# A hybrid block of layers: block 0's states ahead of block 1's turning, maxima in three pairs of PSUM banks in turn, one mix of the last mixer later

## The chip, the core and the metric

The kernel runs on one core of one Trainium2 chip. A core has five engines that run at the same time, each with its own in-order queue: TensorE (PE, matrix products and transposes; its weight loads are listed as PEld), VectorE (DVE), ScalarE (ACT), GpSimd (POOL), and SyncE (SP), which here only issues transfers. They meet in semaphores. PE writes its results into PSUM, eight banks of 128 partitions x 512 float32. The metric is the device time of one execution in microseconds (us); lower is better.

## The reference, cut to what matters

Input is `x` of 2 sequences x 2048 tokens x 256 channels. Four layers follow, each added to its input:

```
x = x + ssm(layernorm(x))                # a = -softplus(A_diag); state = a*state + B u; LN(gelu(C state + D u))
x = x + ffn(layernorm(x))                # channel mixer: sigmoid(r) * (relu(k)^2 @ Wv), tokens mixed with the one before
x = x + attention(layernorm(x))          # 16 heads of 64, causal, K and V from a latent of rank 128
x = x + ffn(layernorm(x))                # the same mixer again
```

## The kernel before

A class `Plan` writes one list of tasks in program order, and five functions (`tensor_program`, `vector_program`, `scalar_program`, `gpsimd_program`, `sync_program`) walk the same list; each engine does its share of every task, in that order. So the list sets the order on every engine at once, and an engine that waits in one task holds up all later tasks of its own.

Tokens are cut into 8 blocks of 512 (4 per sequence), and a block into 4 tiles of 128.

**First layers** (`first_layers`): rounds k = 0 to 10. Round k computes the state-space layer of block k (`ssm_states`: product on PE, scan on DVE; `ssm_output`: product on PE, Gelu on ACT, then `g_stats` on DVE), the end of that layer for block k-1 (`tail_norm` on ACT and POOL, `tail_add` on DVE and POOL), and the first mixer for blocks k-2 and k-3. `ssm_normal` (ACT) and `ssm_front` (PE transposes, ACT copies) prepare a block for `ssm_states`. `stats(...)` adds per tile two DVE instructions (L917, L919) and then one root for all of them (`inverse_std`: DVE L944, ACT L1126, DVE L946 and L949). Ahead of round 0 come `stats(0)`, normal and front of block 0, `ssm_setup` (softplus of `A_diag`: two DVE instructions, Exp and Ln on ACT at L1143 and L1145, two DVE instructions), `stats` of blocks 1 to 3, and normal and front of block 1. In round 0 `stats` of blocks 4 to 7 stands between `ssm_states` 0 and `ssm_output` 0. ACT must load a table before a function that the loaded one doesn't hold (ACT_TABLE_LOAD rows).

**Attention** (`attention`): a unit is one sequence b, one pair of heads p, one block of 512 queries j: 64 units, in that order, so j runs 0 to 3 within a pair of heads. A step is one tile of 128 keys of a unit; unit j has 4(j+1) steps, and the loop takes two steps at a time ("a turn of the loop" below). A turn adds:
- `maximum` (640 in all, about two per turn, for units some 20 steps ahead): two matmuls of q against k (L834) into a pair of banks, then DVE's largest value per row (L1070 for full tiles; L1067 with the causal mask for those on the diagonal);
- two `score` tasks: 8 matmuls each (L857 to L863) into banks (0, 1) and (2, 3); the exponential on ACT (L1287) empties them;
- `filler`: the most urgent of the other products (latent, query, key, value, turned tiles, turned maxima, projections), mostly into bank 7, sometimes into bank 0;
- `weigh` for the two steps of the turn before (L878, PE into bank 4, `heads_out`) and `accumulate` (L1372, POOL, the sum of the exponentials);
- `minus_max`, `denominators`, `invert`, `scale_out`, `two_parts`, `project` of a unit around its end.

All maxima go into banks 5 and 6 (`two_heads`). So a maximum waits until DVE is through with the one before (semaphore `emptied5`). A turn adds one maximum ahead of the scores, one behind them, more in a `while` loop where many are due (units with few steps, above all at the start), and one behind the `weigh` tasks. The next turn's scores may follow directly.

**Last mixer** (`last_mixer`): its first tasks are put into the last turns of attention by the table `ahead`, which counts steps from the end: at -10 `mix_tokens` of block 0, at -6 of block 1 (4 scaled copies on ACT at L1186, 4 instructions on DVE at L1010), at -4 `turn_normal` of block 2. Behind attention, blocks follow with `products`, `square`, `x_stats`, `turn`, `update` and the stores.

The planner gives out banks in `take`: it keeps for each bank the last task that used it, and PE waits for that task's emptying before it writes the bank again:

```
entries.append((g, free, mark))
...
elif kind == "maximum":
    self.take(task, (5, 6))
elif kind == "score":
    n = 2 * (self.step_of[task[1:]] % 2)
    ...
    self.take(task, (n,), (n + 1,))
```

## Time and profile before

| | us |
|---|---|
| median of 3 runs | 2138.2 (2132.14 to 2140.27) |
| the profiled execution, its own time | 2138.73 |
| its span, first to last instruction | 2137.4 |
| PE busy | 1974.2 (92%) |
| DVE busy | 1347.1 (63%) |
| ACT busy | 1100.0 (51%) |
| POOL busy | 1426.1 (67%) |
| mean granted clock of PE | 0.977 of full |

Busy times are of one profiled execution. The span falls into the first layers (to about 250 us), the start of attention (to about 440), the attention loop proper (to about 2040) and the last mixer. A row of the timeline gives start, duration, engine, line, operation, shapes, count, and in square brackets the time that the engine sat idle before it and what released it. Starts of matmuls are more exact than their ends, which are modelled.

### The profile page before, as it was taken

Reading aid. Unit: us, or ns where it says so; the run is one execution under the profiler, and the core shown is the slowest. Engines: PE = TensorE matmul, PEld = TensorE weight load, DVE = VectorE, ACT = ScalarE, POOL = GpSimd, SP = SyncE. Lnnn points to the kernel's source line nnn. Section 1 sums busy time; section 2 is a strip of 40 time slices with the busy share of each in tenths; the row PEclk is TensorE's granted clock in tenths of the full one; section 3 lists DMA queues with packets and bytes.
Section 4 is the critical chain, followed back from the end, with each engine's and each line's share of the span. In section 5 each row is a group of like instructions: output and inputs, shape, how many; then the busy total and the mean of one; then the engine's idle time right before and its main releaser. Section 6 shows DMA issues by size and latency. Waiting matters only on the chain.

```text
span 2137.4 us, 34866 instructions
## 1 busy us (share of the span) xinstructions
PE 1974.2 (92%) x12720; PEld 1223.4 (57%) x12720; DVE 1347.1 (63%) x2719; ACT 1100.0 (51%) x2234; POOL 1426.1 (67%) x812
## 2 busy tenths in 40 slices
PE   4999568999999999999989999999999999999899
PEld 3666445555555555556555665555556555555466
DVE  4888646576657565766655657576656575656443
ACT  4776634445444444445455454445454445454575
POOL 0343314778687868786858687868787878687822
PEclk9999779999999999999999999999999999999999
DMA  3000000000000000000000000000000000000001
GB/s 122 1 1 1 0 7 6 20 11 17 12 20 11 17 11 20 12 17 13 18 11 17 11 20 11 17 12 19 11 18 11 20 12 17 11 14 11 25 25 60
DMA packets 29242, 36.99 MB, mean 17 GB/s; under 512 B 6928, under 2 KB 20368, under 8 KB 29072
## 3 DMA queue, kind: packets, MB, share of 16 engines
q1 hardware_dynamic: 29072, 34.76, 5.3%
q8 instruction: 103, 1.69, 0.3%
q14 instruction: 67, 0.55, 0.1%
HBM read 30.02 MB, written 4.46 MB: 16 GB/s over the span
## 4 chain that ended last, share of the span: by engine, by line
PE 60%; DVE 16%; POOL 13%; ACT 6%; issue 5%; DMA 0%; POOLq 0%; ACTq 0%; DVEq 0%; SPq 0%
PE heads_out L878 16%; POOL acc L1372 11%; PE beside L695 9%; PE two_heads L834 7%; PE scores L695 6%; PE scores L857 4%; PE scores L863 4%; PE scores L859 4%; PE scores L861 4%; DVE part_max L1070 3%; ACT prob L1287 2%; PE beside L889 2%; DVE stats L917 2%; PE two_heads L695 2%; DVE wQK_lo L1031 1%
## 5 line engine op out<-in xcount | busy, mean ns | idle before, releaser
L1372 POOL TENSOR_TENSOR acc<-acc,prob 128x1024 f32<-128x1024 f32 (+3 forms) x512 | 1018.2, 1989 | 207.4 <-ACT prob L1287 151.8
L1287 ACT ACTIVATE prob<-scores 128x512 f32<-128x512 f32 (+3 forms) x1280 | 579.4, 539 | 641.3 <-PE scores L863 290.2
L1070 DVE TENSOR_REDUCE part_max<-two_heads 128x2 f32<-128x1024 f32 x384 | 469.4, 1222 | 279.0 <-PE two_heads L834 278.3
L878 PE MATMUL heads_out<-prob,V 128*64 128x512 f32 (+3 forms) x2560 | 544.3, 546 | 0.0
L1067 DVE CUSTOM_DVE_ANT_0 two_heads<-two_heads,mask 128x128 f32<-128x128 f32 (+3 forms) x512 | 242.2, 515 | 187.2 <-PE two_heads L834 187.1
L834 PE MATMUL two_heads<-k_hi,q_hi 64*128 64x512 f32 (+3 forms) x1280 | 274.6, 424 | 63.9 <-DVE part_max L1070 34.0
L878 PEld LDWEIGHTS heads_out<-prob,V 128*64 128x64 f32 x2560 | 156.8, 137 | 233.4 <-issue 210.4
L834 PEld LDWEIGHTS two_heads<-k_hi,q_hi 64*128 64x128 f32 x1280 | 121.0, 185 | 256.7 <-issue 130.8
L857 PE MATMUL scores<-q_hi,k_hi 64*128 64x512 f32 (+3 forms) x1280 | 236.7, 365 | 1.6 <-ACT neg_max L1274 0.8
L859 PE MATMUL scores<-q_hi,k_lo 64*128 64x512 f32 (+3 forms) x1280 | 235.6, 363 | 0.0
L863 PE MATMUL scores<-neg_max,sel 64*128 64x512 f32 (+3 forms) x1280 | 235.6, 362 | 0.0
L861 PE MATMUL scores<-q_lo,k_hi 64*128 64x512 f32 (+3 forms) x1280 | 235.5, 362 | 0.0
L1367 POOL TENSOR_TENSOR acc<-prob 128x768 f32<-128x768 f32 (+1 forms) x64 | 144.0, 2250 | 98.4 <-ACT prob L1287 97.5
L1381 POOL TENSOR_TENSOR oT_lo<-oT,oT_hi 128x512 fp32r<-128x512 f32 x62 | 79.5, 1282 | 108.7 <-ACT oT_hi L1304 108.4
L861 PEld LDWEIGHTS scores<-q_lo,k_hi 64*128 64x128 f32 x1280 | 122.3, 186 | 18.9
L863 PEld LDWEIGHTS scores<-neg_max,sel 64*128 64x128 f32 x1280 | 122.4, 186 | 18.7
L857 PEld LDWEIGHTS scores<-q_hi,k_hi 64*128 64x128 f32 x1280 | 122.1, 186 | 18.6 <-issue 5.5
L859 PEld LDWEIGHTS scores<-q_hi,k_lo 64*128 64x128 f32 x1280 | 122.2, 186 | 17.5
L1080 DVE TENSOR_TENSOR scores<-scores,limit 128x256 f32<-128x256 f32 x256 | 103.3, 428 | 32.2 <-PE scores L863 31.3
L1377 POOL TENSOR_TENSOR oT<-oT,rden 128x512 f32<-128x512 f32 x62 | 79.4, 1280 | 11.7 <-DMA rden<-rden_rows 11.7
L1298 ACT ACTIVATE den_rows<-beside 128x256 f32<-128x256 f32 x63 | 24.2, 384 | 113.9 <-PE beside L889 113.9
L1333 POOL TENSOR_TENSOR X<-X,gatea 128x512 f32<-128x512 f32 x16 | 20.2, 1278 | 88.7 <-DVE gatea L1018 88.7
(299 smaller groups left out, 2911.8 us busy)
## 6 DMA issues: line engine op xcount, KB each, us to landing
rden<-rden_rows SPq DMA_DIRECT2D x128, 128.0 KB, 2.9
X<-u SPq DMA_DIRECT2D x8, 512.0 KB, 9.0
out<-X SPq DMA_DIRECT2D x8, 512.0 KB, 2.9
wQK_raw<-wQuery SPq DMA_DIRECT2D x16, 192.0 KB, 2.9
wO_raw<-wOut SPq DMA_DIRECT2D x16, 128.0 KB, 2.8
wV_raw<-wValue SPq DMA_DIRECT2D x8, 128.0 KB, 2.7
den<-den_rows SPq DMA_DIRECT2D x64, 4.0 KB
rden_rows<-den SPq DMA_DIRECT2D x64, 4.0 KB, 1.3
```

The costliest lines, as they stand in the source:

```text
L695: made = pe.matmul(dst, l, r, start=first and n == 0, stop=last and n == len(pairs) - 1)
L834: made = pe.matmul(two_heads[:, h, 0:width], q[head(h), t * P:(t + 1) * P], k[head(h), 0:width], start=True, stop=True)
L857: pe.matmul(bank(task, h)[:, x0:], k_hi[g][head(h), kc], q_hi[i][head(h), x0:], start=True, stop=False)
L859: pe.matmul(bank(task, h)[:, x0:], k_lo[g][head(h), kc], q_hi[i][head(h), x0:], start=False, stop=False)
L861: pe.matmul(bank(task, h)[:, x0:], k_hi[g][head(h), kc], q_lo[i][head(h), x0:], start=False, stop=False)
L863: pe.matmul(bank(task, h)[:, x0:], sel[head(h), :], neg_max[idx % NMAX][head(h), x0:], start=False, stop=True).then_inc(full(task, h)[0], 1)
L878: made = pe.matmul(heads_out[head(h), x0:], V[vn % NVS][:, tt, p % 2, head(h)], prob[step % NPROB][:, h, x0:], start=t == 0, stop=t == TPB ...
L1067: made = ve.tensor_tensor_reduce(out=two_heads[:, h, 0:width], in0=two_heads[:, h, 0:width], in1=mask[:, BLK - width:], scale=1.0, scalar= ...
L1070: made = ve.reduce_max(part_max[:, t, :, c:c + 1], two_heads[:, :, 0:width], AX.X)
L1287: ac.activation(prob[step % NPROB][:, h, x0:], bank(task, h)[:, x0:], ACT.Exp).then_inc(empty(task, h)[0], 1)
L1367: po.tensor_tensor(total[:, :, x0:], old[:, :, x0:], new[:, :, x0:], ALU.add).then_inc(acc_ok, 1)
L1372: po.tensor_tensor(total[:, :, x0:], total[:, :, x0:], new[:, :, x0:], ALU.add).then_inc(acc_ok, 1)
```

## The change

Four things, all in the order of the tasks or in the banks:

1. `ssm_setup` is split. `ssm_log` (two DVE instructions, Exp, Ln) is the first task of the program; `ssm_decay` (the last two DVE instructions) stands behind the front of block 0. `A_diag` gets a semaphore of its own (`diag_in`), and the wait for the initial state moves to the scan.
2. In the first layers, normal and front of block 1 move behind `ssm_states` 0; `mixer_weights` to round 1; `stats` of blocks 4 to 7 from ahead of `ssm_output` 0 to behind the front of block 2.
3. A `maximum` whose predecessor among the tasks with a bank is a `maximum` too takes the next pair of three: (5, 6), (0, 1), (2, 3); any other takes (5, 6). `weigh` has no bank in this sense. Of the 640 maxima 583 stay in (5, 6), 55 go to (0, 1) and 2 to (2, 3). In 48 of the 57 two `weigh` tasks lie between the two maxima, and the next task on PE is a `score` in banks (0, 1); these are spread over units 6 to 63. The other nine lie among units 1 to 4. The `while` loop also adds a filler behind each of its maxima, which changes the order among units 1 to 3 and nowhere else.
4. `mix_tokens` of block 1 of the last mixer moves from step -6 to 0, behind the last `weigh`.

The diff, cut to its core:

```
@@ Plan.add
         elif kind == "maximum":
-            self.take(task, (5, 6))
+            before = next((x[0] for x in reversed(self.tasks[:-1]) if x in self.bank), None)
+            self.max_banks = (self.max_banks + 1) % 3 if before == kind else 0
+            self.take(task, ((5, 6), (0, 1), (2, 3))[self.max_banks])
@@ Plan.first_layers
+        self.add("ssm_log")
         stats(0)
         self.add("ssm_normal", 0)
         self.add("ssm_front", 0)
-        self.add("ssm_setup")
+        self.add("ssm_decay")
         stats(*range(1, NBLK))
-        self.add("ssm_normal", 1)
-        self.add("ssm_front", 1)
-        self.add("mixer_weights", "a")
         for k in range(NBL + 3):
...
             if k < NBL:
                 self.add("ssm_states", k)
+            if k == 0:
+                self.add("ssm_normal", 1)
+                self.add("ssm_front", 1)
+            if k == 1:
+                self.add("mixer_weights", "a")
...
-            if k == 0:
-                stats(*range(NBLK, NBL))
             if k + 2 < NBL:
                 self.add("ssm_normal", k + 2)
             if k < NBL:
                 self.add("ssm_output", k)
             if k + 2 < NBL:
                 self.add("ssm_front", k + 2)
+            if k == 0:
+                stats(*range(NBLK, NBL))
@@ Plan.attention
-                 -6: [("mix_tokens", "b", 1)], -4: [("turn_normal", "b", 2)]}
+                 -4: [("turn_normal", "b", 2)], 0: [("mix_tokens", "b", 1)]}
...
             while self.at < goal - 1:
                 maximum()
+                filler(10 ** 6)
@@ vector_program
-                elif kind == "ssm_setup":
-                    w.wait_ge(small_in, 48)
+                elif kind == "ssm_log":
+                    w.wait_ge(diag_in, 16)
...
+                elif kind == "ssm_decay":
                     w.wait_ge(soft_a, 2)
@@ sync_program
-            sp.dma_start(a_in[:, :], aDiag).then_inc(small_in, 16)
+            sp.dma_start(a_in[:, :], aDiag).then_inc(diag_in, 16)
```

How the instructions stand on the engines. ACT at the very start of the program (`std` is the root of the variances, `xn` the normalised tiles, `xT` a turned block, `a_log` the softplus), before:

```order
L1126 ACT_TABLE_LOAD
L1126 ACTIVATE std<-std 128x4
L1119 ACTIVATE xn<-X,minus_mean,rstd 128x256 x4
L1140 ACTIVATE xT<-scores 128x512 x2
L1143 ACT_TABLE_LOAD
L1143 ACTIVATE a_log<-a_abs 128x2
L1145 ACT_TABLE_LOAD
L1145 ACTIVATE a_log<-a_log 128x2
L1126 ACT_TABLE_LOAD
L1126 ACTIVATE std<-std 128x12
```

and now:

```order
L1156 ACT_TABLE_LOAD
L1156 ACTIVATE a_log<-a_abs 128x2
L1158 ACT_TABLE_LOAD
L1158 ACTIVATE a_log<-a_log 128x2
L1139 ACT_TABLE_LOAD
L1139 ACTIVATE std<-std 128x4
L1132 ACTIVATE xn<-X,minus_mean,rstd 128x256 x4
L1153 ACTIVATE xT<-scores 128x512 x2
L1139 ACTIVATE std<-std 128x12
```

The softplus has moved from behind block 0's turned copies to ahead of its root, and one table load is gone.

PE in the attention loop, at one of the 48 places: two maxima of unit 10 (the second is for its key block 1, queries 0 to 127), two `weigh` tasks of unit 7 between them, and the score of unit 7, step 12, behind them. `emptied5` counts what DVE is through with in banks 5 and 6, `emptied0` and `emptied1` what is read out of banks 0 and 1. Before:

```order
L834 MATMUL two_heads<-k_hi,q_hi 128x512 [waits emptied5]
L834 MATMUL two_heads<-k_hi,q_hi 128x512
L878 MATMUL heads_out<-prob,V 64x512 x4
L834 MATMUL two_heads<-k_hi,q_hi 128x512 [waits emptied5]
L834 MATMUL two_heads<-k_hi,q_hi 128x512
L857 MATMUL scores<-q_hi,k_hi 128x512 [waits emptied1,emptied0]
L857 MATMUL scores<-q_hi,k_hi 128x512
```

and now:

```order
L845 MATMUL two_heads<-k_hi,q_hi 128x512 [waits emptied5]
L845 MATMUL two_heads<-k_hi,q_hi 128x512
L889 MATMUL heads_out<-prob,V 64x512 x4
L845 MATMUL scores<-k_hi,q_hi 128x512 [waits emptied1,emptied0]
L845 MATMUL scores<-k_hi,q_hi 128x512
L868 MATMUL scores<-q_hi,k_hi 128x512 [waits emptied0]
L868 MATMUL scores<-q_hi,k_hi 128x512
```

The order is the same; the second maximum has moved into the banks of the score that follows it, and that score's `emptied0` now counts DVE's reading of the maximum.

DVE at the end of attention (`oT_lo` belongs to unit 62's output, L1080 is the mask on the scores of the last steps, L1113 adds a projection to X), before:

```order
L1105 TENSOR_TENSOR oT_lo<-oT,oT_hi 128x512
L1010 SCALAR_TENSOR_TENSOR mixb<-xTFb,mub,mixb 128x512 x4
L1080 TENSOR_TENSOR scores<-scores,limit 128x2x128 x2
L1113 TENSOR_TENSOR X<-X,beside 128x512 x2
L1080 TENSOR_TENSOR scores<-scores,limit 128x2x128 x2
L917 BN_STATS stats<-X 128x6
```

and now:

```order
L1118 TENSOR_TENSOR oT_lo<-oT,oT_hi 128x512
L1093 TENSOR_TENSOR scores<-scores,limit 128x2x128 x2
L1126 TENSOR_TENSOR X<-X,beside 128x512 x2
L1093 TENSOR_TENSOR scores<-scores,limit 128x2x128 x2
L1023 SCALAR_TENSOR_TENSOR mixb<-xTFb,mub,mixb 128x512 x4
L928 BN_STATS stats<-X 128x6
```

The four mixing instructions have moved behind the last masks.

## Rows read from the trace of the kernel before

**Rows 1.** The page: span, PE's busy time, the chain that ended last by engine.

```profile
span 2137.4 us, 34866 instructions
...
PE 60%; DVE 16%; POOL 13%; ACT 6%; issue 5%; DMA 0%; POOLq 0%; ACTq 0%; DVEq 0%; SPq 0%
```

**Rows 2.** By stretch: length, busy PE, PEld, DVE, ACT, POOL, clock, DMA, GB/s.

```profile
440.00:2060.00 1620.00, 1555.21 (x10796) 937.06 (x10793) 1024.52 (x2043) 814.51 (x1726) 1240.99 (x675) 0.99 0.05 15
```

**Rows 3.** Transfers issued at 3.7 to 5 us: count, KB each, us to landing.

```profile
X<-u SPq DMA_DIRECT2D x3, 512.0 KB, 9.7
```

**Rows 4.** Timeline of the first 50 us: start, us, engine, line, [idle before].

```profile
7.31 0.20 ACT L1126 ACTIVATE std<-std 128x4 f32<-128x4 f32 x1 [5.29 <-DVE std L944]
...
12.06 1.28 ACT L1143 ACT_TABLE_LOAD   x1
...
15.11 0.16 DVE L958 SCALAR_TENSOR_TENSOR a_col<-a_in,a_log 128x2 f32<-128x2 f32 x1 [6.91 <-ACT a_log L1145]
...
21.89 0.17 DVE L944 TENSOR_SCALAR std<-mean_var 128x12 f32<-128x12 f32 x1
...
29.56 1.28 DVE L973 TENSOR_TENSOR_SCAN xs<-decay,state,heads_out 128x512 f32<-128x512 f32 x1 [6.71 <-PE heads_out L695]
...
45.41 0.43 DVE L917 BATCH_NORM_STATS2 stats<-G 128x6 f32<-128x256 f32 x1 [3.41 <-ACT G L1154]
...
48.81 2.07 ACT L1119 ACTIVATE nrm<-G,minus_mean,rstd 128x256 f32<-128x256 f32 x4 [0.44 <-DVE minus_mean L949]
```

**Rows 5.** Waits of PE from 440 to 2000 us: total, times, longest.

```profile
PE two_heads L834 <- DVE part_max L1070: 22.9, 38, 2.5
PE two_heads L834 <- DVE part_max L1067: 15.9, 31, 1.2
```

**Rows 6.** Timeline, PE and DVE, the full-width place quoted above.

```profile
531.83 1.94 PE L878 MATMUL heads_out<-prob,V 128*64 128x512 f32 x8
...
533.70 0.50 PE L834 MATMUL two_heads<-k_hi,q_hi 64*128 64x512 f32 x2
...
534.04 0.39 PE L857 MATMUL scores<-q_hi,k_hi 64*128 64x512 f32 x2
...
534.24 1.23 DVE L1070 TENSOR_REDUCE part_max<-two_heads 128x2 f32<-128x1024 f32 x1 [1.08 <-PE two_heads L834]
```

**Rows 7.** The same 10 us later, a maximum of 128 keys.

```profile
543.91 0.45 PE L857 MATMUL scores<-q_hi,k_hi 64*128 64x512 f32 x2
...
544.58 0.14 DVE L1067 DVE_READ_ACCUMULATOR2_ANT part_max<- 128x1 f32 x1
```

**Rows 8.** Timeline of PE: a maximum that waited for the one before it.

```profile
334.00 0.49 PE L834 MATMUL two_heads<-k_hi,q_hi 64*128 64x512 f32 x2 [1.32 <-DVE part_max L1070]
```

**Rows 9.** Timeline of PE: the maximum that follows one of the 48 places.

```profile
675.05 0.50 PE L834 MATMUL two_heads<-k_hi,q_hi 64*128 64x512 f32 x2 [0.45 <-DVE part_max L1070]
```

**Rows 10.** Timeline of PE behind a stretch in which POOL adds back to back.

```profile
758.50 0.49 PE L834 MATMUL two_heads<-k_hi,q_hi 64*128 64x512 f32 x2 [0.46 <-DVE part_max L1067]
```

**Rows 11.** Timeline of PE behind one of the longest waits of the loop.

```profile
1077.36 1.08 PE L780 MATMUL beside<-ident,att_xn 128*128 128x128 f32 x4 [1.96 <-ACT att_xn L1119]
1078.37 2.78 PE L878 MATMUL heads_out<-prob,V 128*64 128x512 f32 x8
```

**Rows 12.** By stretch, around that wait (columns as in rows 2).

```profile
1075.00:1080.00 5.00, 3.04 (x10) 1.32 (x12) 2.72 (x8) 3.49 (x9) 1.99 (x2) 0.71 0.00 0
```

**Rows 13.** Timeline of PE at the start of attention.

```profile
316.41 0.50 PE L834 MATMUL two_heads<-k_hi,q_hi 64*128 64x512 f32 x2 [1.50 <-DVE q_lo L1053]
```

**Rows 14.** Timeline of DVE, PE and ACT at the end of attention.

```profile
2027.22 4.84 DVE L1010 SCALAR_TENSOR_TENSOR mixb<-xTFb,mub,mixb 128x512 f32<-128x512 f32 x4
...
2033.38 0.58 PE L695 MATMUL beside<-wO_hi,oT_hi 128*128 128x256 f32 x1 [3.11 <-DVE X L1113]
...
2041.31 1.98 PE L695 MATMUL two_heads<-mixb,wFb 128*128 128x512 f32 x4 [0.70 <-ACT oT L1293]
...
2051.72 0.21 ACT L1126 ACTIVATE std<-std 128x12 f32<-128x12 f32 x1
```

More of the change, by code:

```diff
@@ L516, in full, with two_banks @@
             return filled[b], n
+        def two_banks(task):
+            first = plan.bank[task][0][0][0]
+            return two_heads[:, :, :] if first == 5 else scores[:, first:first + 2, :]
         def empty(task, i=0):
@@ L523, in build @@
         x_in = [sem(f"x_in{i}") for i in range(NBL)]
-        small_in, wA_in, mu_in, wF_in, kd_in, wQK_in, wV_in, wO_in, stored = (
-            sem(s) for s in ("small_in", "wA_in", "mu_in", "wF_in", "kd_in", "wQK_in", "wV_in", "wO_in", "stored"))
+        diag_in, small_in, wA_in, mu_in, wF_in, kd_in, wQK_in, wV_in, wO_in, stored = (
+            sem(s) for s in ("diag_in", "small_in", "wA_in", "mu_in", "wF_in", "kd_in", "wQK_in", "wV_in", "wO_in", "stored"))
         ident_zero, ident_ok, att_fill, att_const, masked = (
@@ L833, in tensor_program @@
                     for h in range(2):
-                        made = pe.matmul(two_heads[:, h, 0:width], q[head(h), t * P:(t + 1) * P], k[head(h), 0:width], start=True, stop=True)
+                        made = pe.matmul(two_banks(task)[:, h, 0:width], q[head(h), t * P:(t + 1) * P], k[head(h), 0:width], start=True, stop=True)
                     made.then_inc(full(task)[0], 1)
@@ L967, in vector_program @@
                         w.wait_ge(decay_ok, 1)
+                        w.wait_ge(small_in, 32)
                         if i >= 2:
```

12 lines of the change are left out of this document (6 added, 6 removed).

## The prediction

> **What bounds the kernel now.** I read the page first. The chain that ended last runs on PE for 60%, and on DVE and POOL for most of the rest [rows 1]. The table by stretch says how to take that: in the attention loop PE is busy 1555.2 of 1620 us at a clock of 0.99 [rows 2]. PE works in order, so there its time is its work plus its waits, and whoever makes it wait sets the end. The list of its waits is short: 38.8 us in 69 waits are for DVE's reading of a maximum [rows 5], and the rest of the list comes to 17 us. So a new wait of PE in the loop is paid in full unless it swallows one of these few. The first 50 us are another regime: no engine is full, and DVE's line of statistics, roots and scans sets the pace, with waits of 6.91 us for the softplus, 6.71 for the first states and 3.41 for the first Gelu [rows 4]. At the end of attention PE waits 3.11 us for DVE once [rows 14].
>
> **The start.** DVE's second group of statistics (blocks 1 to 3) now begins behind the softplus, which sits behind block 0's copies and two table loads of 1.28 us [rows 4]. With the softplus first, Exp can run when `A_diag` is there, about when block 0 of X is; Ln's and the root's table loads then stand ahead of block 0's root, which I put 1.0 us later than 7.31 us. DVE reaches block 1 at 9.4 us. The transfers now bound it: block 3 lands about 9.7 us behind its issue at some 4.2 us [rows 3], so near 14, and 4 tiles at 0.53 us give the root at 16.8 instead of 21.89 us [rows 4]: 5.1 us gained. Then the states of block 0 need no more waiting for block 1 on ACT and PE: PE has had their products since 12.5 us, so the wait of 6.71 us shrinks to nothing. The 16 tiles of blocks 4 to 7 (8.5 us) and block 0's own statistics follow, and the wait of 3.41 us for Gelu becomes a wait for the root of blocks 4 to 7, which on ACT now sits behind Gelu and the front of block 2: about 4 us. Step by step that puts the first `tail_norm` at 36.7 us instead of 48.81: **12 us gained**. What follows is a closed cycle of rounds without outside input, so the shift is passed on. Bounds: 16 us if the root doesn't wait, 5 if only the first step comes through.
>
> **The start of attention.** The added fillers put `latent` 2 and `query` 2 between three maxima that wait for DVE, where before they ran behind them and waited for their own copies [rows 13]. Counting on with the same durations, unit 2's first maximum comes 2.3 us earlier than 316.41, and the later fillers leave holes of 1 to 2 us less. I take **4 us gained**, between 0 and 8.
>
> **The banks, where two maxima touch (nine places, units 1 to 4).** Before, the second waits some 1.3 us for DVE [rows 8], and the score follows it 0.34 us later. Now the second runs at once, but the score behind it needs banks 0 and 1, so it waits until DVE has read both. DVE reads them one after the other (1.23 us each [rows 6]), so PE ends up waiting for two readings instead of one, with only its own 0.5 us hidden: 0.4 to 1.2 us lost at five places, and gained only where three stand in a row (1.5 and 0.4 us). Sum: **3 us lost**.
>
> **The banks, where weighing lies between (48 places).** This term decides. At 533.70 us a maximum starts without any wait, since 1.94 us of weighing covered DVE's reading of the one before; the score starts at 534.04 in other banks; DVE reads the maximum from 534.24 to 535.47 beside it [rows 6]. In the changed kernel that maximum lies in banks 0 and 1, and the order shows the score waiting on `emptied0`, which now counts DVE's reading. So it can't start before 535.47 + 0.04. The first matmul behind a wait takes 0.50 instead of 0.39 us [rows 6, 8]. Together 1.47 + 0.11 = 1.58 us. Of the 48 places 34 are alike, DVE being through 1.43 or 1.44 us after the score's start in each: 34 x 1.58 = 53.7. In the other 14 the maximum has 128 keys; DVE is through at 544.72, 0.81 us after the score at 543.91 [rows 7], so 0.9 us each: 12.6. ACT has emptied both banks before the maximum wants them in all 48, so that wait costs nothing. Nothing else can run on PE meanwhile.
>
> What comes back: at 5 places the maximum itself had waited for the one before, and 0.54 us each returns (2.7); behind 7 places, where the scores are short, the next maximum waited 0.45 us for DVE [rows 9] and won't (3.2); and in 12 stretches the chain runs on POOL's back-to-back additions, behind which PE had waited 0.46 us (eight alike [rows 10], two 1.0): 5.6. Hence 66.3 - 11.5 = **55 us lost**. The bounds: 45, if POOL's stretches swallow both of their waits partly, and 68 for the clock, below.
>
> A rule of the Trainium skill speaks for the change: in Perfetto Trace Analysis, section Matmuls, independent groups should rotate through PSUM banks, so that one's evacuation overlaps the next one's products. The rows show a rotation into banks that the very next product needs, which removes an overlap. By the rule alone the waits of the nine places (1.3 us for each that had one) and the 2.7 us above would go, some 10 us, and nothing would be lost.
>
> **The end.** Four mixing instructions, 4.84 us on DVE, stand ahead of two masks and an addition for which PE waits 3.11 us [rows 14]. Moved behind the last masks they free PE: projection, the last scores, exponentials and weighing all come 3.3 us sooner, and so do the first products at 2041.31. The mixing then takes 2.6 us on ACT and 2.7 on DVE behind attention. The products of block 1 need it only some 5 us later. The statistics behind it on DVE end at about 2047.9, and ACT, which took their root only at 2051.72 [rows 14], would be free for it at about 2048.4. So it stays hidden: **3.3 us gained**, between 1 and 4.
>
> **Sum.** Against the execution's own 2138.7 us (span 2137.4 and 1.3 around it): -12 - 4 + 3 + 55 - 3.3 = +38.7, so 2177.4 us; the median of the runs shown, 2138.2, is 0.5 lower. I say **2177 us**.
>
> **The rivals.**
> *The waits are covered* (faster). PE's place in the loop might be slack where I call it the bound: POOL is busy 1241 of 1620 us [rows 2] and holds 13% of the chain [rows 1]. If each added wait were swallowed by a later one of PE, only the gains would be left: 2138.7 - 12 - 4 - 3.3 = 2119 us, or 2109 if PE's old waits for maxima went as well. It decides the sign if a wait costs less than 19.3 / 48 = 0.40 us. Against it: behind each POOL stretch PE had waited only 0.46 us [rows 10], so POOL leads it by no more, and all waits of the loop together are some 56 us, most of them in [rows 5]. The bank rule named above would end here.
> *The clock falls.* Behind a wait of 1.96 us eight weighing matmuls took 2.78 instead of 1.94 us, and the 5 us around it had a clock of 0.71 [rows 11, 12], so part of it at 1.2 instead of 2.4 GHz: about 1.5 us more. The new waits are 1.3 us, like that of 334.00, behind which nothing was slow [rows 8]. Seven times two of them come within 4 us; should the clock fall there, 10 us are added (2187), and at all 34 full-width places 50 us (2228).
> The Trainium skill knows such a case, in TensorE: Matmul & The Clock Gate, section A second HAM failure mode: psum-queue depth-cycling: small idles between groups, while banks are cycled, move the clock between its levels. Here that would be the 2228 us.
> *The start's gain is lost in the rounds.* If a later round waits for something that doesn't shift, up to 12 us are missing: 2189. For it: ACT's order in round 0 puts a root behind Gelu. Against: behind the last load of X the rounds take nothing from outside.
> *Some waits are cheaper*, say half of them, because POOL's stretches hold two each: 2150, about the same as before to a percent.
>
> **How the numbers follow.** My sum with its bounds 0.66; the start's gain missing 0.09; the clock falling widely 0.09; half the waits covered 0.08; covered nearly or wholly 0.08. The time is that of the first, 2177. Its terms at their ends, not all on one side, give 2160 to 2200. To hold 8 in 10 the range must reach the half-covered case too: 2150 to 2200. A measurement of this kernel tells about 0.5% (10.7 us) from no change. Faster by more than that is the covered case, 0.08; within it falls a part of the half-covered one, 0.05; slower 0.87.
>
> **What would show it.** In the profile of the changed kernel: PE's waits at the first score matmul (L868) for DVE's maxima, some 48 in the loop, at 1.3 and 0.7 us, 55 to 65 us in total, where the row of before had none; the loop longer by some 55 us at the same PE busy time; the first `tail_norm` root near 37 us; no wait of 3.11 us near the end. I am wrong if that new row is there and the loop isn't longer by at least 30 us (then POOL was the bound), if clocks under 0.95 show in the loop, or if the first `tail_norm` lies later than 44 us.

## The result and the profile after

The changed kernel takes **2188.7 us** (median of 6 runs, 2184.35 to 2196.57) where the kernel before took 2138.3 (6 runs beside it, 2132.14 to 2140.27): ratio **1.0246, 95% interval 1.0222 to 1.027**. It is slower by some 50 us. The forecast was 2177 in 2150 to 2200; the sign and the mechanism of the main term hold, and the sum is 12 us short.

The page of after: span, busy time, the chain by engine, and the group of the first score matmul (busy, mean ns, idle time before and its releaser).

```profile
span 2185.7 us, 34868 instructions
...
PE 1989.4 (91%) x12720; PEld 1225.4 (56%) x12720; DVE 1346.7 (62%) x2719; ACT 1099.0 (50%) x2233; POOL 1424.9 (65%) x812
...
PE 72%; DVE 17%; ACT 5%; issue 3%; POOL 2%; DMA 0%; ACTq 0%; DVEq 0%; SPq 0%; POOLq 0%
...
L868 PE MATMUL scores<-q_hi,k_hi 64*128 64x512 f32 (+3 forms) x1280 | 242.6, 374 | 69.8 <-DVE part_max L1083 53.3
```

The other engines' work is the same to a few us. Against [rows 1], PE's share of the chain is larger, DVE's nearly as before and POOL's gone from 13% to 2%.

The same work in both kernels, from maximum 56 to maximum 639, by stretch (columns as in rows 2), first the kernel before:

```profile
428.74:1978.35 1549.61, 1496.25 (x10482) 902.50 (x10481) 996.41 (x1991) 766.98 (x1638) 1202.19 (x656) 1.00 0.05 15
```

and after:

```profile
418.04:2030.00 1611.96, 1507.99 (x10481) 902.94 (x10481) 998.64 (x1991) 766.87 (x1638) 1201.24 (x656) 0.99 0.05 14
```

The stretch is 62.35 us longer, PE's busy time in it by 11.7: 50.6 us are new waiting, the rest slower matmuls. PE's waits in that stretch of after (total us, times, longest):

```profile
PE scores L868 <- DVE part_max L1083: 45.0, 34, 1.3
PE two_heads L845 <- DVE part_max L1083: 17.1, 27, 2.5
PE two_heads L845 <- DVE part_max L1081: 16.2, 31, 1.2
PE scores L868 <- DVE part_max L1081: 9.9, 14, 0.7
PE beside L900 <- DVE k_lo L1071: 7.7, 13, 0.8
...
PE scores L845 <- ACT prob L1300: 2.4, 4, 0.6
```

The first and the fourth row are new: 48 waits, 54.9 us, one at each place where weighing lies between two maxima. The old waits [rows 5] fell only from 38.8 us (in nearly the same stretch) to 33.3. The last row is new too, and the prediction had it at nothing.

The place of [rows 6] in after, timeline of PE and DVE:

```profile
527.54 1.94 PE L889 MATMUL heads_out<-prob,V 128*64 128x512 f32 x8
529.41 0.51 PE L845 MATMUL scores<-k_hi,q_hi 64*128 64x512 f32 x2
531.24 0.50 PE L868 MATMUL scores<-q_hi,k_hi 64*128 64x512 f32 x2 [1.32 <-DVE part_max L1083]
...
529.96 1.23 DVE L1083 TENSOR_REDUCE part_max<-scores 128x2 f32<-128x1024 f32 x1 [1.08 <-PE scores L845]
```

The maximum is now written to `scores`, DVE reads it until 531.19, and the score starts 1.83 us behind the maximum where it had started 0.34 behind. With 128 keys (the place of [rows 7]) the wait is 0.70:

```profile
542.08 0.50 PE L868 MATMUL scores<-q_hi,k_hi 64*128 64x512 f32 x2 [0.70 <-DVE part_max L1081]
```

The start, timeline of ACT and DVE, which answers to [rows 4]:

```profile
5.64 1.28 ACT L1158 ACT_TABLE_LOAD   x1
6.94 0.20 ACT L1158 ACTIVATE a_log<-a_log 128x2 f32<-128x2 f32 x1
7.16 1.28 ACT L1139 ACT_TABLE_LOAD   x1
8.45 0.20 ACT L1139 ACTIVATE std<-std 128x4 f32<-128x4 f32 x1
...
15.97 0.17 DVE L955 TENSOR_SCALAR std<-mean_var 128x12 f32<-128x12 f32 x1
...
16.85 1.28 DVE L986 TENSOR_TENSOR_SCAN xs<-decay,state,scores 128x512 f32<-128x512 f32 x1
...
30.31 0.25 DVE L957 RECIPROCAL rstd<-std 128x16 f32<-128x16 f32 x1 [1.77 <-ACT std L1139]
...
33.98 0.60 ACT L1132 ACTIVATE nrm<-G,minus_mean,rstd 128x256 f32<-128x256 f32 x1 [0.44 <-DVE minus_mean L960]
```

The first `tail_norm` comes at 33.98 instead of 48.81 us, and 14.8 us is the shift of everything up to 247 us. The end, timeline of PE, against [rows 14]:

```profile
2079.18 0.56 PE L706 MATMUL beside<-wO_hi,oT_hi 128*128 128x256 f32 x1 [3.09 <-DVE oT_lo L1118]
...
2080.73 3.68 PE L889 MATMUL heads_out<-prob,V 128*64 128x512 f32 x8
2084.34 0.58 PE L706 MATMUL beside<-wO_hi,oT_hi 128*128 128x256 f32 x1
...
2086.57 2.37 PE L889 MATMUL heads_out<-prob,V 128*64 128x512 f32 x16
2089.64 1.98 PE L706 MATMUL two_heads<-mixb,wFb 128*128 128x512 f32 x4 [0.70 <-ACT oT L1306]
```

The wait of 3.11 us ahead of the projection (now at 2084.34) is gone, but eight weighing matmuls ahead of it took 3.68 instead of 1.94 us.

I followed each of the 640 maxima through both traces: the delay of after against before at each of them. It is -14.8 us in the first layers, -16.3 at maximum 0, -10.7 at maxima 46 and 56, +51.7 at maximum 639, and +48.3 at the end. In the loop it grows in steps: 28 of 1.57 to 1.71 us (44.9), 20 of 0.90 to 0.98 (18.7), and -1.2 for all the rest together.

### The profile page after: what moved, and what is told of

The parts are those of the page before. It is cut to its first block, busy times and chain, and to the rows that moved or that the text cites. A ratio compares the mean times of both kernels' runs of the same rounds, so it can differ in the third digit from the quotient of the medians.

```text
span 2185.7 us, 34868 instructions
## 1 busy us (share of the span) xinstructions
PE 1989.4 (91%) x12720; PEld 1225.4 (56%) x12720; DVE 1346.7 (62%) x2719; ACT 1099.0 (50%) x2233; POOL 1424.9 (65%) x812
## 4 chain that ended last, share of the span: by engine, by line
PE 72%; DVE 17%; ACT 5%; issue 3%; POOL 2%; DMA 0%; ACTq 0%; DVEq 0%; SPq 0%; POOLq 0%
PE heads_out L889 21%; PE beside L706 11%; PE two_heads L845 7%; PE scores L706 6%; PE scores L868 6%; DVE part_max L1083 5%; PE scores L874 5%; PE scores L870 5%; PE scores L872 5%; ACT prob L1300 2%; PE beside L900 2%; PE two_heads L706 2%; DVE wQK_lo L1044 1%; DVE stats L928 1%; PE beside L853 1%
## 5 line engine op out<-in xcount | busy, mean ns | idle before, releaser
L1083 DVE TENSOR_REDUCE part_max<-two_heads 128x2 f32<-128x1024 f32 x345 | 421.7, 1222 | 275.7 <-PE two_heads L845 275.1
L1081 DVE CUSTOM_DVE_ANT_0 two_heads<-two_heads,mask 128x256 f32<-128x256 f32 (+3 forms) x476 | 230.7, 526 | 174.6 <-PE two_heads L845 174.4
L868 PE MATMUL scores<-q_hi,k_hi 64*128 64x512 f32 (+3 forms) x1280 | 242.6, 374 | 69.8 <-DVE part_max L1083 53.3
L845 PE MATMUL two_heads<-k_hi,q_hi 64*128 64x512 f32 (+3 forms) x1166 | 248.5, 422 | 40.9 <-DVE part_max L1083 20.1
L845 PEld LDWEIGHTS two_heads<-k_hi,q_hi 64*128 64x128 f32 x1166 | 110.7, 185 | 195.6 <-issue 130.6
L870 PEld LDWEIGHTS scores<-q_hi,k_lo 64*128 64x128 f32 x1280 | 122.8, 187 | 15.9
L1126 DVE TENSOR_TENSOR X<-X,beside 128x512 f32<-128x512 f32 x80 | 54.5, 682 | 38.7 <-PE beside L706 38.2
```

The source lines that it names most:

```text
L845: made = pe.matmul(two_banks(task)[:, h, 0:width], q[head(h), t * P:(t + 1) * P], k[head(h), 0:width], start=True, stop=True)
L868: pe.matmul(bank(task, h)[:, x0:], k_hi[g][head(h), kc], q_hi[i][head(h), x0:], start=True, stop=False)
L870: pe.matmul(bank(task, h)[:, x0:], k_lo[g][head(h), kc], q_hi[i][head(h), x0:], start=False, stop=False)
L1081: made = ve.tensor_tensor_reduce(out=scored, in0=scored, in1=mask[:, BLK - width:], scale=1.0, scalar=MASKED, op0=ALU.add, op1=ALU.max, ac ...
L1083: made = ve.reduce_max(part_max[:, t, :, c:c + 1], two_banks(task)[:, :, 0:width], AX.X)
```

## The experiments

Ratios are against the kernel before, run beside each. From a ratio to us I multiply by 2137; for the difference of two ratios the half-widths of their intervals are added in squares. Each run has one trace, and single executions of one kernel differ by up to 17 us (last section), so sizes are taken from medians or from stretches of the trace in which nothing else differs.

### The banks

**after_old_banks**, the changed kernel with

```
-            before = next((x[0] for x in reversed(self.tasks[:-1]) if x in self.bank), None)
-            self.max_banks = (self.max_banks + 1) % 3 if before == kind else 0
-            self.take(task, ((5, 6), (0, 1), (2, 3))[self.max_banks])
+            self.take(task, (5, 6))
```

> The changed kernel with every maximum back in banks 5 and 6, so the start, the fillers and the end are as changed, the banks as before. My theory (PE is the bound of the loop, and each score that follows a maximum in banks 0 and 1 pays for DVE's reading of it): the row of PE at the first score matmul waiting for DVE's maximum (43.6 us in 33 waits, and 9.2 in 13) is gone, the stretch from maximum 56 to maximum 639 is some 62 us shorter, and the time is 2119 to 2124 us. Rival (the loss comes from the new order of the fillers or of the start, which shifts POOL's and DVE's work against PE's, and the banks are paid for by slack): 2165 to 2189 us, and the row is gone all the same.

Measured: **2109.3 us, ratio 0.9878 (0.9863 to 0.9893)**. This is faster than both kernels, and 10 us under the range that I had expected. The rotation costs 1.0246 - 0.9878 = 3.7%, 79 +- 6 us. In the trace the 48 steps are gone.

**banks_alone**, the kernel before with these three lines the other way round.

> The kernel before with the rotation of the maxima's banks and nothing else. My theory: 34 full-width places at 1.58 us and 14 of 128 keys at 0.9, less what comes back, plus about 8 us at the nine places where two maxima touch: 2138 + 62 to 74 = 2200 to 2212 us, with the same row of waits at the score as in the changed kernel. Rival (the waits at the score only show at this size because the other parts changed what stands before them): under 2180 us. A second question of this run: where two maxima touch, before every part of the change, does the rotation alone lose 3 us, as I predicted, or 8?

Measured: **2206.4 us, ratio 1.0328 (1.0312 to 1.0345)**, some 70 us lost. The trace has the same steps (28 of 1.60, 20 of 0.94 us, sum 63.8) and the same two rows of waits at the score, 44.9 us in 34 and 9.8 in 14. From maximum 0 to 46 it loses 7.7 us, so the 3 us predicted for the nine touching places were too few whatever stands around them.

**touching_only**, the changed kernel with weighing counted as a break, which puts the 48 places back:

```
-            before = next((x[0] for x in reversed(self.tasks[:-1]) if x in self.bank), None)
+            before = next((x[0] for x in reversed(self.tasks[:-1]) if x in self.bank or x[0] == "weigh"), None)
```

> The changed kernel, but weighing between two maxima counts as a break, so the 48 places use banks 5 and 6 again and only maxima that touch on PE take turns. My theory: this takes back all of the loop's 66 us and leaves what the touching places cost beside the fillers, about 6 us by the traces: 2109.3 + 6 = 2113 to 2118 us. Rival (the 48 places are not what costs): over 2150 us.

Measured: **2124.7 us, ratio 0.9957 (0.9941 to 0.9973)**. So the 48 places cost 1.0246 - 0.9957 = 2.9%, 62 +- 6 us, where the steps of the trace say 63.6. What is left, 0.9957 - 0.9878, is 17 +- 5 us against the old banks, more than I expected here too. The two traces are 15.7 us apart: 1.0 by maximum 0, 10.7 between maxima 0 and 46, where the touching places are, and 4.0 in the loop behind, where both kernels run the same instructions. So the touching places themselves account for some 11 of the 17 us, clock included; that the rest is due to them isn't shown.

Why so much shows at maximum 18. With the old banks (after_old_banks), timeline of PE:

```profile
316.90 0.50 PE L843 MATMUL two_heads<-k_hi,q_hi 64*128 64x512 f32 x2 [1.32 <-DVE part_max L1081]
317.24 0.40 PE L866 MATMUL scores<-q_hi,k_hi 64*128 64x512 f32 x2
317.47 0.39 PE L868 MATMUL scores<-q_hi,k_lo 64*128 64x512 f32 x2
```

and in the changed kernel, PE, then DVE:

```profile
317.30 0.79 PE L868 MATMUL scores<-q_hi,k_hi 64*128 64x512 f32 x2 [2.10 <-DVE part_max L1083]
317.89 0.63 PE L870 MATMUL scores<-q_hi,k_lo 64*128 64x512 f32 x2
...
314.56 1.22 DVE L1083 TENSOR_REDUCE part_max<-two_heads 128x2 f32<-128x1024 f32 x1
...
315.69 0.41 DVE L1052 TENSOR_TENSOR wO_lo<-wO_raw,wO_hi 128x256 fp32r<-128x256 f32 x1
316.02 1.22 DVE L1083 TENSOR_REDUCE part_max<-scores 128x2 f32<-128x1024 f32 x1
```

From the first maximum (314.01 us, and 315.08 with the old banks) to the score it is 3.29 us instead of 2.16, as DVE reads both and does a piece of 0.41 us between: 1.1 us, the upper end of my 0.4 to 1.2. From the score to the next maximum it is 3.29 instead of 1.85, because behind the wait of 2.10 us a matmul takes 0.63 instead of 0.39 us. In the 3 us from 317.3 the granted clock is 0.51, the lower level of 1.2 GHz. This 1.4 us was in no term.

**second_score_banks**, the changed kernel with the spare pairs in the other order:

```
-            self.take(task, ((5, 6), (0, 1), (2, 3))[self.max_banks])
+            self.take(task, ((5, 6), (2, 3), (0, 1))[self.max_banks])
```

> The changed kernel with the two spare pairs of banks taken in the other order: 5 and 6, then 2 and 3, then 0 and 1. At the 48 places with weighing in between, the maximum then lies in banks 2 and 3, and the next score in 0 and 1 doesn't need them, only the score behind it (rows of before: that one starts 0.93 us behind the first). My theory (the loss is the reading that a score must wait for, so it depends on which score needs the banks and not on the rotation as such): 28 full-width places cost 1.60 - 0.93 = 0.67 us instead of 1.60, the 20 others nothing instead of 0.93: 63.6 falls to about 19, so the time is 2188.7 - 45 - some us at the nine touching places = 2135 to 2146 us. Rival (a maximum in any bank of the scores costs the same, for instance because DVE's reading of it is late in every case): 2180 to 2195 us.

Measured: **2142.1 us, ratio 1.0034 (1.002 to 1.0048)**, 45 +- 6 us less than the changed kernel, as expected. The place of [rows 6] in it, timeline of PE:

```profile
523.75 0.50 PE L845 MATMUL scores<-k_hi,q_hi 64*128 64x512 f32 x2
524.10 0.39 PE L868 MATMUL scores<-q_hi,k_hi 64*128 64x512 f32 x2
...
525.58 0.45 PE L868 MATMUL scores<-q_hi,k_hi 64*128 64x384 f32 x2 [0.39 <-DVE part_max L1083]
```

The first score follows at once, the second still waits. The full-width steps are 0.63 to 0.71 us, and behind a maximum of 128 keys there is none. At the places with short scores the step is mostly 0.5, and at five of the seven another 0.45 to 0.73 us stands just ahead of it, since the maximum there waits longer for ACT to empty banks 2 and 3 (1.27 us at maximum 550, where it had waited 0.57 for DVE). So the price is set by how soon the next products need the banks, and this is the clearest evidence for the mechanism: same rotation, same number of banks, other order.

**touching_second** is touching_only with `((5, 6), (2, 3))` and the count modulo 2, so that the second of two touching maxima lies where the next score does not.

> As touching_only, but the second of two touching maxima lies in banks 2 and 3, which the score right behind it doesn't need, and a third one in 5 and 6 again. If my account of the banks is right in both directions, this keeps what the rotation was to bring: up to 1.3 us at each touching place that had waited and no new wait for the score behind it: 2109.3 - 2 to - 8 = 2101 to 2108 us. If DVE's pace and not the banks sets these first maxima, the waits only move one product on: 2109 to 2113 us.

Measured: **2112.1 us, ratio 0.9893 (0.9873 to 0.9913)**: 3 +- 5 us above the old banks. The loss of the touching places is gone, and no gain takes its place. At maximum 18 the 1.32 us are no longer ahead of the maximum but ahead of the second score:

```profile
316.99 0.39 PE L845 MATMUL scores<-k_hi,q_hi 64*128 64x512 f32 x2
317.34 0.50 PE L868 MATMUL scores<-q_hi,k_hi 64*128 64x512 f32 x2
...
319.94 0.49 PE L868 MATMUL scores<-q_hi,k_hi 64*128 64x512 f32 x2 [1.41 <-DVE part_max L1083]
```

At the start of attention DVE has to read each maximum in turn anyway, so a free pair of banks only moves the wait. This also bears on the rule of the Trainium skill that the prediction weighed (Perfetto Trace Analysis, section Matmuls: rotate independent groups through banks). Of the 10 us that the rule would give, some 7 belong to the touching places; even with a rotation that removes no overlap there they did not show. The 2.7 us in the loop were not tried in this run.

### The start, the fillers, the end

**start_alone**, the kernel before with points 1 and 2 of the change (the split of `ssm_setup`, and the order of the first layers).

> The kernel before with the logarithm first and block 0's states ahead of block 1's turning, nothing else. My theory: the first root of tail_norm comes 14 to 15 us sooner (at some 34 us) and the whole of it arrives at the end: 2138 - 15 = 2121 to 2126 us. Rival (the rounds of the first half or the loop have slack, so part of it is waited away again before the last store): 2130 to 2138 us, with the shift against before shrinking somewhere between 50 us and the last maximum.

Measured: **2121.2 us, ratio 0.9937 (0.9922 to 0.9952)**, 13.5 +- 3 us gained. The first `tail_norm` is at 34.09 us. In its trace 16.2 us are there at maximum 0, 11.7 at maximum 18, and 12.4 at maximum 639. So the first layers pass the shift on whole, and the 4.5 us lost go at the start of attention (below).

**softplus_alone**, the kernel before with

```
+        self.add("ssm_log")
         stats(0)
         self.add("ssm_normal", 0)
         self.add("ssm_front", 0)
-        self.add("ssm_setup")
+        self.add("ssm_decay")
```

> The kernel before with the logarithm ahead of the first statistics and nothing else; block 0's states still stand behind block 1's turning. My prediction: the root of blocks 1 to 3 comes 5.1 us sooner than 21.89 us (the profile of the changed kernel says 5.9), and as no later step waits for anything else the first tail_norm (48.81 us before) comes about 5 to 6 us sooner too: 2130 to 2134 us where before has 2135 to 2138. Rival (the wait of 6.71 us for the first states grows by what the root gains, since ACT's and PE's work for block 1 stands there): within 2 us of before.

Measured: 2134.3 us, ratio 0.9975 (0.9955 to 0.9995), 5 +- 4 us gained. The root of blocks 1 to 3 is 6.1 us earlier than before, the first `tail_norm` at 42.07 us, 6.7 earlier. It is passed on as expected: 7.3 us are there at every maximum from 0 to 56. (Its profiled execution was its fastest, 2119.8 us, so its trace gains more later on.)

**order_alone**, the kernel before with the rest of the change at the start:

```
-        self.add("ssm_normal", 1)
-        self.add("ssm_front", 1)
-        self.add("mixer_weights", "a")
...
+            if k == 0:
+                self.add("ssm_normal", 1)
+                self.add("ssm_front", 1)
+            if k == 1:
+                self.add("mixer_weights", "a")
```

and `stats` of blocks 4 to 7 behind the front of block 2.

> The kernel before with block 0's states ahead of block 1's turning and the statistics of blocks 4 to 7 behind the front of block 2, the logarithm where it was. The root of blocks 1 to 3 stays at some 22 us; the wait of 6.71 us for the first states goes, so the first scan starts near 22.9 instead of 29.56 us; the wait for Gelu becomes one for the root of blocks 4 to 7. My theory (the two halves of the start add up, 14.8 - 5.9 = 9 us for this one): first tail_norm near 40 us, 2126 to 2130 us. Rival (they cover each other, so that either alone brings most of it or none): first tail_norm at 34 to 36 or later than 45 us.

Measured: 2135.1 us, ratio 0.9983 (0.9969 to 0.9997), 3.6 +- 3 us gained, less than I expected (8 to 12). Yet the first `tail_norm` is at 40.77 us, 8.0 earlier, and 6.7 + 8.0 is the 14.8 of both. In this execution 8.5 us are still there at maximum 10, 4.0 at maximum 18 and 1.4 at maximum 46, so most of it is lost at the start of attention. The medians of the two halves add up to 9 +- 5 us, against 13.5 +- 3 for both; they neither show nor rule out that the halves add up.

What happens there is seen by putting the kernels side by side in which PE has the same instructions between maxima 10 and 18:

| | maximum 10 to 18, us |
|---|---|
| before | 27.75 |
| end_alone | 27.75 |
| softplus_alone | 27.76 |
| start_alone | 32.23 |
| order_alone | 32.23 |
| half_sums (below) | 32.23 |

In these six executions there are two lengths and nothing between. The timeline of PE says why, first before, then start_alone (the query's products behind the same wait of 1.41 us):

```profile
313.24 0.51 PE L695 MATMUL beside<-att_xT_hi,wQK_hi 128*128 128x512 f32 x1 [1.41 <-DVE lat_lo L1049]
313.58 0.40 PE L695 MATMUL beside<-att_xT_lo,wQK_hi 128*128 128x512 f32 x1
```

```profile
297.09 0.79 PE L703 MATMUL beside<-att_xT_hi,wQK_hi 128*128 128x512 f32 x1 [1.41 <-DVE lat_lo L1059]
297.69 0.63 PE L703 MATMUL beside<-att_xT_lo,wQK_hi 128*128 128x512 f32 x1
```

The granted clock is 1.00 in the first stretch and 0.50 in the second. The matmuls before it are the same and as slow (0.63 us each) in both; no row shows what decided it. With one trace for each kernel it is also open whether the outcome changes from execution to execution or goes with the kernel.

**fillers_alone**, the kernel before with

```
             while self.at < goal - 1:
                 maximum()
+                filler(10 ** 6)
```

> The kernel before with the fillers between the first maxima and nothing else. My prediction gave it 4 us gained (0 to 8); the medians so far leave some 26.0 - 13.5 - 4.7 = 8 us for it, the traces 5 to 6: 2128 to 2134 us where before has 2135 to 2138. Rival (the fillers help only because the start has shifted what they wait for): within 2 us of before.

Measured: 2130.8 us, ratio 0.9983 (0.997 to 0.9997), 3.6 +- 3 us gained. My 4 us hold. Counted from maximum 0, unit 2's first maximum (number 12) comes 2.5 us earlier, where I had said 2.3; in this execution it is all lost again by maximum 46, 2.3 us of it at maximum 44. Whether the fillers gain more behind the new start stays open: against start_alone, no_end below gives 6 +- 6 us.

**end_alone**, the kernel before with

```
-                 -6: [("mix_tokens", "b", 1)], -4: [("turn_normal", "b", 2)]}
+                 -4: [("turn_normal", "b", 2)], 0: [("mix_tokens", "b", 1)]}
```

> The kernel before with the mixing of block 1 put behind the last masks, nothing else. My theory: PE's wait of 3.11 us near 2033 goes, the first products of the last mixer come 3.3 us sooner and so does the end: 2134 to 2136 us, and the trace's last 100 us are 3.3 us shorter. Rival (the mixing is then late for the products of block 1, and PE waits there): within 1 us of before, with a new wait of PE for mixb.

Measured: 2131.9 us, ratio **0.9978 (0.9968 to 0.9988)**, 4.7 +- 2.1 us gained. That is 2 us under the range that I had expected; my 3.3 us lie in the interval, and PE has no wait for `mixb`.

**no_end**, the changed kernel with the old banks and this line undone.

> The changed kernel with the old banks and without the change at the end: start and fillers alone. The end's share is then the difference to the changed kernel with the old banks (0.9878 of before). My theory, 3.3 us from the wait that goes: ratio 0.9893, 2112 to 2115 us. From end_alone it was 4.7 with an interval of 2.6 to 6.8. Rival (the wait of 3.1 us near the end goes but the products behind the wait ahead of it then run at the low clock, so half is given back): 0 to 2 us, ratio 0.988.

Measured: 2118.6 us, ratio 0.991 (0.9888 to 0.9933); against after_old_banks the end is worth 7 +- 6 us. Neither theory is ruled out by this run alone; taken together with end_alone, the gain lies between 3 and 7 us. The end is decided between maximum 639 and the last mixer's first products; from there on it is 96.1 us in every trace. That way is 62.7 to 63.0 us in before, start_alone, order_alone, fillers_alone and no_end, but 60.5 in banks_alone and 57.7 in softplus_alone, which don't have this change either; with it, 59.6 (after), 57.3 (touching_second), 56.1 (end_alone) and 55.9 (after_old_banks). Two pairs in which the clock behind PE's wait for POOL (14.7 us behind maximum 639) is alike, and the weighing behind the first wait of 3.1 us is slow in both, differ by 0.9 (banks_alone, after) and 1.5 (softplus_alone, end_alone). So the wait I took away is 3.1 us only where the matmuls ahead of it run at full clock. Where they don't, only 0.7 (banks_alone) or 1.5 us (softplus_alone) of it are left to take away. And where it is whole the low clock comes behind it: in before the last 16 weighing matmuls take 3.76 us, in after 2.37.

### Does POOL bind?

**half_sums**, the kernel before with

```
-                        po.tensor_tensor(total[:, :, x0:], total[:, :, x0:], new[:, :, x0:], ALU.add).then_inc(acc_ok, 1)
+                        po.tensor_tensor(total[:, :, x0:(BLK + x0) // 2], total[:, :, x0:(BLK + x0) // 2], new[:, :, x0:(BLK + x0) // 2], ALU.add).then_inc(acc_ok, 1)
...
-                    ac.activation(den_rows[:, :], bank(task)[:, 0:BLK // 2], ACT.Copy).then_inc(empty(task)[0], 1)
+                    ac.activation(den_rows[:, :], bank(task)[:, 0:BLK // 2], ACT.Copy, bias=1.0).then_inc(empty(task)[0], 1)
```

> The kernel before with POOL's additions for the denominators cut to half their columns from the third key tile of each unit on (the other half isn't added, and 1 is added to each denominator so that none is zero): this leaves out part of the computation of the denominators. Everything else is as before, PE's work too. My theory (PE is the bound, and the 13% that the chain of before shows on POOL only runs beside PE): POOL's busy time falls by 400 us or more and the time by less than 10 us, 2126 to 2138. Rival (POOL's back-to-back stretches bind part of the loop): the time falls by 20 us or more, and the steps are at those stretches.

Measured: **2105.4 us, ratio 0.9846 (0.9824 to 0.9868)**, 33 +- 5 us less. My theory of this run falls. The stretch from maximum 56 to 639 (columns as in rows 2) and PE's waits in it:

```profile
435.97:1962.24 1526.27, 1489.92 (x10481) 902.01 (x10481) 973.41 (x1991) 766.77 (x1638) 788.07 (x657) 1.00 0.05 15
```

```profile
PE two_heads L834 <- DVE part_max L1070: 16.9, 32, 0.8
PE two_heads L834 <- DVE part_max L1067: 14.0, 29, 1.2
PE beside L780 <- ACT att_xn L1119: 2.0, 1, 2.0
```

It is 23.3 us shorter, PE's busy time by 6.3 (less slow clock), its waits by 17. One row is gone as a whole: 13 waits of the denominators' matmul, 7.4 us, which the profile of before puts down to DVE's `k_lo` (the denominators go into the bank that `k_lo` is read from). The profile is right in that: at all 13, `k_lo` ends 0.06 us ahead of the matmul, and the last addition that POOL had finished ended 0.75 us before that. What POOL does is to hold up DVE. One of the 13 in before, timeline of DVE, POOL and PE:

```profile
1530.95 1.29 DVE L1031 TENSOR_TENSOR wQK_lo<-wQK_raw,wQK_hi 128x128 fp32r<-128x128 f32 x1
1532.16 0.68 DVE L1058 TENSOR_TENSOR k_lo<-beside,k_hi 128x512 fp32r<-128x512 f32 x1
...
1529.71 2.38 POOL L1372 TENSOR_TENSOR acc<-acc,prob 128x1024 f32<-128x1024 f32 x1 [0.51 <-ACT prob L1287]
...
1532.90 0.64 PE L889 MATMUL beside<-acc,ones 128*32 128x256 f32 x8 [0.56 <-DVE k_lo L1058]
```

and in half_sums:

```profile
1519.82 0.26 DVE L1031 TENSOR_TENSOR wQK_lo<-wQK_raw,wQK_hi 128x128 fp32r<-128x128 f32 x1
...
1518.58 1.29 POOL L1372 TENSOR_TENSOR acc<-acc,prob 128x512 f32<-128x512 f32 x1 [0.51 <-ACT prob L1287]
...
1521.13 0.64 PE L889 MATMUL beside<-acc,ones 128*32 128x256 f32 x8
```

DVE's subtraction of 128x128 starts while an addition of POOL runs and ends 0.15 us behind the addition's end, at all 14 such places of before's loop: it takes 1.27 to 1.51 us. Beside the halved additions it takes 0.26 to 0.41. `k_lo` stands behind it, so it is late, and PE waits. DVE's whole busy time in the stretch falls by 23 us with the same 1991 instructions, while its reading of a maximum takes 1.22 us in both. The rest of the 17 us are waits for DVE as well (for full maxima 23.5 to 16.9, for masked ones 15.9 to 14.0, for turned tiles 2.8 to 1.8); the longest, 2.5 us at 1493.89 in before, stands behind a DVE instruction of 128x16 that took 2.32 us beside an addition.

Another 13.5 us go behind maximum 639, where each unit's end (additions, denominators, scaling, projection) has no other work beside it; they include slow clock too. (Between maxima 0 and 46 this execution had lost 7.1 us to before, by the longer stretch above and more like it.)

So POOL does hold PE, for a part of its time, and in the loop mostly through DVE. But it does not swallow the new waits. In the changed kernel the row of 13 waits is still there with 7.7 us (the list of PE's waits above), though PE had become 62 us slower. The traces show why: POOL's addition moves with PE. At 12 of the 14 places it starts 1.03 to 1.25 us ahead of DVE's subtraction in before, and at the same distance to 0.02 us in after. That it does so because it needs the exponentials, which need PE's products, I take from the order of the work; no run tests it by itself.

## Why the prediction came out as it did

By its terms, us (negative: gained); medians where a run isolates the term:

| term | predicted | measured |
|---|---|---|
| start | -12 | -13.5 +- 3; -14.8 in the trace |
| start of attention, fillers | -4 | -3.6 +- 3 |
| nine touching places | +3 | +17 +- 5, of which 8 to 11 lie there in traces |
| 48 places | +55 | +62 +- 6; 63.6 in the trace |
| end | -3.3 | -4.7 +- 2.1 |
| sum | +38.7 | +56.9; the changed kernel itself +52.6 +- 5 |

**What bounds.** Right, and it carries the forecast: PE has no slack in the loop, each of the 48 waits arrived in full at the end. *The waits are covered* is out: it needed under 0.40 us a place, and they cost 1.60 and 0.94. (Its 2109 us for PE's old waits gone as well took off only the 10 us of the bank rule, where [rows 5] have 38.8 us; this changes nothing in the forecast.)

**The price of a place.** Right to a few hundredths: 1.58 predicted and 1.60 measured, 0.9 and 0.92, and 0.97 at six of the seven places with short scores, where I had taken off 0.45 from 1.58.

**What comes back.** This step failed. I had counted 5.6 us as given back behind POOL's stretches, because the chain ran on POOL there; none of it came: the 31 waits for a maximum with the causal mask, of the kind of [rows 10], are 16.2 us where they were 15.9. The chain's 13% on POOL were no slack of PE, and half_sums shows POOL's part to be another one: its additions make DVE late. Why the chain ran on POOL there, and does so by only 2% in after, no run explains. I had also counted 2.7 us at 5 places where a maximum had itself waited for the one before. At one of them (maximum 230) 0.7 us came back; at the other four the maximum waits as long for ACT to empty banks 0 and 1 (2.4 us in 4 waits), which I had put at nothing. At two of these four the clock fell as well and added 1.4 and 0.6 us (behind maximum 471 eight weighing matmuls took 3.25 us, in before 1.72); at the five other places with short scores 0.19 us each came back behind. Without the 8.3 us of this step the term would have been 66.3 - 3.2 = 63.1, against 63.6.

**The touching places.** At maximum 18, the one worked through here, the wait was sized right at its upper end (1.1 us), but the low clock behind it was missing (1.4 us). I had a row for it, the 2.78 us behind a wait of 1.96 [rows 11], and worked out its price only for the loop. DVE's other pieces between the two readings make the wait 2.1 us.

**The clock.** As a rival with a wide fall at all full-width places it is out. With 48 waits of up to 1.3 us the loop's clock is 0.99. Of its stretches of 5 us, 7 are under 0.95, where before there were 5; PE's busy time is 11.7 us longer, of which 48 x 0.11 = 5.3 are the first matmuls behind the waits. Of the seven cases of two waits within 4 us, which I had priced at 10 us, the clock fell at two, for 2 us. My sign that I would be wrong if clocks under 0.95 show in the loop was badly chosen, as before shows them too. The Trainium skill's case for it (TensorE: Matmul & The Clock Gate, section A second HAM failure mode: psum-queue depth-cycling) is thus not this loop's; by these rows it is nearer at the start of attention, where idle and work alternate.

**The start.** Right in mechanism, 3 us too careful in one number: DVE's wait for the root of blocks 4 to 7 is 1.77 us where I had put about 4. The root of blocks 1 to 3 began at 15.97 us (16.8 predicted, though 4.2 + 9.7 + 4 x 0.53 is 16.0). The transfers did not bound it: DVE waited only 0.1 us for one (block 2), and block 3 had landed at 13.07 us, 0.7 ahead of DVE's turn for it; it was DVE's 12 tiles of 0.53 us from 9.26 us on. No later round took the shift back, but at the start of attention the low clock can (4.5 us in start_alone's trace). *The start's gain is lost in the rounds* is out by start_alone.

**The end.** The wait of 3.11 us is gone and the mixing is hidden, as said. How much of it reaches the end depends on the clock ahead of it, which I had not considered; the median is in my 1 to 4 us or just above.

So 2177 was low by 12 us for two reasons: 8.3 us counted as returned that did not return, and the touching places, at 3 us, lacked the low clock behind their waits (5 to 8 us by the traces, more by the medians). The start, which gave 1.5 to 3 us more than forecast, hides a part of both.

## What to carry to other kernels

Rotating through more banks helps only if the banks rotated into are not those that the very next product writes: list for each use who writes the bank next and how soon, and price the wait by the reader's end minus that start. On an engine without slack such a wait is paid in full, and another engine's share in the chain does not say that it will absorb it; halve that engine's work in a run and look. The name of a releaser says who came last, and not why it was late: look at what ran ahead of it on its own engine, and at durations that differ for one and the same instruction. Time the parts of a change apart: here start, fillers and end together gain 1.2% (2109 us), and three lines of bank choice cost three times that.

## What the runs showed of the hardware that I had not expected

- The granted clock behind one and the same wait is not always the same. Behind a wait of 1.41 us, in the same order of work, it was 1.00 in one kernel and 0.50 in another (0.40 and 0.63 us a matmul), and the stretch around it was 27.75 us in three executions and 32.23 in three others. Behind waits of 3.25 to 3.5 us near the end PE's projection ran at 0.58 or at 0.39 us a first matmul.
- The clock goes with the time of single executions: softplus_alone ran from 2119.8 to 2136.9 us, its two fastest with a mean granted clock of 0.981 and 0.982, the other eight with 0.975 to 0.977. A gain of 3 us can be read from 10 executions, or from a stretch of the trace, but not from one time.
- A subtraction of two tiles on DVE that starts while POOL adds is not just slower: it ends 0.15 us behind POOL's addition, at all 14 places in before and at all 14 in after. So the same instruction takes 1.02 to 1.77 us, where it takes 0.26 to 0.41 in half_sums, whose additions are over sooner. DVE's reading of a maximum out of PSUM takes 1.22 us, whether POOL's additions are whole or halved.
- POOL's additions took 0.73, 1.29, 1.82 and 2.38 us for 256, 512, 768 and 1024 columns in before, and 1.28 for 512 in half_sums: some 0.55 us for each 256 columns, and little besides.
